# One meeting of the engines per stage instead of two, and the first pair of heads split one stage earlier, in a six-stage graph-attention and transformer kernel

## What is computed

```python
output = self_feat                              # [v, q] @ W_self.T + b_self
for d in range(2):
    output = output + _gat_attention(self_feat, cond, vb, Wq[d], bq[d], Wk[d], bk[d], Wout[d], bout[d])
x = v + relu(output)
mod = silu(c) @ W_mod + b_mod
sh_msa, sc_msa, g_msa, sh_mlp, sc_mlp, g_mlp = jnp.split(mod, 6, axis=-1)
x = x + g_msa * _attention(_modulate(_layernorm(x), sh_msa, sc_msa), W_qkv, W_out, b_out)
x = x + g_mlp * _ff(_modulate(_layernorm(x), sh_mlp, sc_mlp), W1, b1, W2, b2)
```

## Time and profile before

| What | Value |
|---|---|
| median of 3 runs | 3193.44 us (3193.24 to 3194.74) |
| the profiled execution | 3194.45 us |
| its span, first to last instruction | 3192.7 us |
| PE, PEld busy | 3071.8 us (96%), 2442.5 us (77%) |
| DVE, ACT, POOL busy | 1852.1 us (58%), 1341.3 us (42%), 845.3 us (26%) |
| mean granted TensorE clock | 0.981 |
| stages by first meeting | tables to 170.3, graph to 511.8, projections to 1062.5, attention to 2238.4, output projection to 2424.9, mlp to 3191.1 us |

### The profile page before, as it was taken

The page is one execution under the profiler, slowest core; times in us unless marked ns, Lnnn a source line. Parts: engine busy times, 40 slices in busy tenths (PEclk is TensorE's granted clock), DMA queues, the critical chain, the costliest instruction groups (busy, mean ns, idle before and its releaser), DMA issues. The chain is left out here.

```text
span 3192.7 us, 62151 instructions
## 1 busy us (share of the span) xinstructions
PE 3071.8 (96%) x24696; PEld 2442.5 (77%) x24696; DVE 1852.1 (58%) x2743; ACT 1341.3 (42%) x2786; POOL 845.3 (26%) x571
## 2 busy tenths in 40 slices
PE   8979998999999799999999999998996999999998
PEld 5969997888888577777777777776785888888887
DVE  4358982221211588888888888887674334343332
ACT  2146662222222377777777777776003111111111
POOL 1011213000000244434443444345455111111110
PEclk9989999999999899999999999999997999999999
DMA  4554322333332433333333333332663001000100
GB/s 141 176 186 149 117 79 99 106 105 114 113 106 93 102 107 92 91 100 81 88 94 100 81 88 88 102 87 68 221 232 112 1 27 33 26 33 26 33 14 14
DMA packets 196341, 297.28 MB, mean 93 GB/s; under 512 B 27888, under 2 KB 105712, under 8 KB 194054
## 3 DMA queue, kind: packets, MB, share of 16 engines
q1 hardware_dynamic: 182528, 276.54, 27.8%
q0 software_dynamic: 4288, 14.68, 1.3%
q10 hardware_dynamic: 9296, 2.77, 0.4%
HBM read 190.44 MB, written 103.49 MB: 92 GB/s over the span
## 5 line engine op out<-in xcount | busy, mean ns | idle before, releaser
L1339 DVE TENSOR_REDUCE b_nm<-b_ps 128x1 f32<-128x1024 f32 x512 | 602.0, 1217 | 16.6 <-PE b_ps L1280 3.4
L1246 ACT ACTIVATE b_p<-b_ps,b_nm 128x1024 f32<-128x1024 f32 x512 | 565.0, 1113 | 41.0 <-DVE b_nm L1339 41.0
L1309 PE MATMUL b_po<-b_pt,b_v 128*64 128x256 f32 x4096 | 498.3, 385 | 0.8 <-DVE b_pt L1359 0.8
L1251 ACT ACTIVATE b_pt<-b_tp_act 128x512 f32<-128x512 f32 x512 | 308.6, 603 | 306.4 <-PE b_tp_dve L1292 306.4
L1359 DVE COPY b_pt<-b_tp_dve 128x512 f32<-128x512 f32 x512 | 351.5, 687 | 117.9 <-PE b_tp_dve L1292 117.9
L1292 PEld LDWEIGHTS b_tp_act<-ident,b_p 64*128 64x128 f32 x4096 | 313.0, 139 | 129.7 <-issue 100.8
L1309 PEld LDWEIGHTS b_po<-b_pt,b_v 128*64 128x64 f32 x4096 | 271.8, 136 | 128.7 <-ACT b_pt L1251 0.9
L1292 PE MATMUL b_tp_act<-ident,b_p 64*128 64x64 f32 x4096 | 348.6, 225 | 2.4 <-issue 2.4
L1292 PE MATMUL b_tp_dve<-ident,b_p 64*128 64x64 f32 x4096 | 348.6, 225 | 0.0
L1701 ACT ACTIVATE d_ge<-d_pf,d_b 128x512 f32<-128x512 f32 x128 | 88.1, 689 | 596.7 <-PE d_pf L1723 596.7
L1292 PEld LDWEIGHTS b_tp_dve<-ident,b_p 64*128 64x128 f32 x4096 | 312.6, 139 | 1.6
(11 more groups left out here) (253 smaller groups left out, 5666.1 us busy)
## 6 DMA issues: line engine op xcount, KB each, us to landing
b_raw_q<-q_t SPq DMA_DIRECT2D x128, 256.0 KB, 4.1
q_t<-p_qk SPq DMA_DIRECT2D x64, 256.0 KB, 2.0
k_t<-p_qk SPq DMA_DIRECT2D x64, 256.0 KB, 2.0
v_n<-p_vs SPq DMA_DIRECT2D x32, 512.0 KB, 3.2
b_raw_k<-k_t SPq DMA_DIRECT2D x128, 128.0 KB, 4.2
b_v<-v_n SPq DMA_DIRECT2D x32, 512.0 KB, 3.9
b_rb<-inv SPq DMA_DIRECT2D x64, 256.0 KB, 3.8
o_t<-b_ot SPq DMA_DIRECT2D x32, 512.0 KB, 2.6
```

The source lines that it names most:

```text
L1246: act.activation(pr[k % 4][:], ps[k % 2][:], ACT.Exp, bias=nm[:, k % 4:k % 4 + 1], accum_out=rs[:, n:n + 1]).then_inc(exp_done, 1)
L1251: act.activation(dst, src, ACT.Copy).then_inc(t_out[0], 1)
L1309: mm = pe.matmul(po[rows, (blk % 2) * 2 * P:(blk % 2 + 1) * 2 * P], vt[u][:, kc, rows], pt[blk % 2][h][:, kc, :], start=(kc == 0), stop=(k ...
L1339: dve.tensor_reduce(nm[:, k % 4:k % 4 + 1], ps[k % 2][:], axis=AX.X, op=ALU.max, negate=True).then_inc(max_done, 1)
```

## The change

`sems()` no longer makes a second meeting. POOL clears the numbers in contiguous ranges right behind the block's own meeting, at the head of its program for the next stage, and the numbers are released so that the next stage takes others. Every block is opened with `no_gpsimd_drain=True`, so POOL's full drain is gone from the meeting. Because of that, the stores of `y` in `graph_attention` move from POOL's queue to SP's: SP issues the store of tile k - 4 ahead of the load of tile k, and waits for the last ones. In `projections`, SP loads q and k of pair 0 at the head of the last group (eight DMAs), DVE splits both heads there, ahead of that group's v copies, and the result stays in tiles `pair0` that `attention` uses as its first set. The load, the split and the wait on them at the start of `attention` are gone, with the semaphores `first_in` and `first_split`.

```diff
-def sems(ctx, nc, prefix, names, first=False):
+def sems(ctx, nc, prefix, names):
...
     def clear():
-        nc.clear_and_free_semaphores(handles)
-        if first:
-            nc.all_engine_barrier()
+        numbers = sorted(h.num for h in handles)
+        for low in [n for n in numbers if n - 1 not in numbers]:
+            high = low
+            while high in numbers:
+                high += 1
+            nc.gpsimd.sem_clear(range(low, high))
+        for h in handles:
+            nc.release_semaphore(h)
...
-        w_mod_in = sems(ctx, nc, "tables", "w_mod_in0 w_mod_in1")
-        block = ctx.enter_context(nc.Block())
+        w_mod_in = [nc.alloc_semaphore("tables_w_mod_in%d" % i) for i in range(2)]
+        for h in w_mod_in:
+            ctx.callback(nc.gpsimd.sem_clear, h)
+        block = ctx.enter_context(nc.Block(no_gpsimd_drain=True))
...
# graph_attention, SP
+            def store(k):
+                sp.wait_ge(y_done, k + 1)
+                sp.dma_start(y[k * P:(k + 1) * P, :], yo[k % 2][:]).then_inc(y_out[k % 2], 16)
+
             def turn(i):
                 for j in range(TT):
                     k = i * TT + j
+                    if k >= 4:
+                        store(k - 4)
                     sp.wait_ge(x_free, k + 1)
...
+            for k in range(B * BT - 4, B * BT):
+                store(k)
+            for n in range(2):
+                sp.wait_ge(y_out[n], 16 * B * BT // 2)
...
# graph_attention, POOL
-                pool.dma_start(y[k * P:(k + 1) * P, :], yo[k % 2][:]).then_inc(y_out[k % 2], 16)
...
-            for n in range(2):
-                pool.wait_ge(y_out[n], 16 * B * BT // 2)
...
# projections, SP
+            def load_pair0():
+                for h in range(2):
+                    for half in range(2):
+                        rows = slice(half * D1, (half + 1) * D1)
+                        sp.dma_start(raw_q[h][rows, :], q_t[0, h * D1:(h + 1) * D1, :]).then_inc(pair_in, 16)
+                        sp.dma_start(raw_k[h][rows, :], k_t[0, h * D1:(h + 1) * D1, half * S // 2:(half + 1) * S // 2]
+                                     ).then_inc(pair_in, 16)
...
+                    if last and hf:
+                        load_pair0()
...
# projections, DVE
+                    if not more:
+                        dve.wait_ge(pair_in, 128)
+                        for h in range(2):
+                            dve.tensor_copy(pair0["qh"][h][:], raw_q[h][:])
+                            dve.tensor_copy(pair0["kh"][h][:], raw_k[h][:]).then_inc(pair_rounded, 1)
+                            dve.wait_ge(pair_rounded, h + 1)
+                            dve.tensor_tensor(pair0["ql"][h][:], raw_q[h][:], pair0["qh"][h][:], ALU.subtract)
+                            dve.tensor_tensor(pair0["kl"][h][:], raw_k[h][:], pair0["kh"][h][:], ALU.subtract)
...
# attention
-        qh = [ring(ctx, nc, f"b_qh{u}", 2, [P, S], F32R) for u in range(2)]
+        qh = [pair0["qh"], ring(ctx, nc, "b_qh", 2, [P, S], F32R)]
...
-                for h in range(2):
-                    for half in range(2):
-                        sp.dma_start(raw_q[h][HALF[half], :], q_t[0, HALF[h], :]).then_inc(first_in[h], 16)
-                        sp.dma_start(raw_k[h][HALF[half], :], k_t[0, HALF[h], half * SK:(half + 1) * SK]
-                                     ).then_inc(first_in[h], 16)
...
-            pool.wait_ge(first_split, 4)
             pool.sem_inc(raw_used, 1)
...
-                if k in (0, 2):
-                    pe.wait_ge(first_split, k + 2)
-                elif s == 0:
+                if k and s == 0:
                     pe.wait_ge(qk_ready, i * TURN + k // STEPS)
...
-            for h in range(2):
-                dve.wait_ge(first_in[h], 64)
-                dve.tensor_copy(qh[0][h][:], raw_q[h][:])
-                dve.tensor_copy(kh[0][h][:], raw_k[h][:]).then_inc(first_split, 1)
-                dve.wait_ge(first_split, 2 * h + 1)
-                dve.tensor_tensor(ql[0][h][:], raw_q[h][:], qh[0][h][:], ALU.subtract)
-                dve.tensor_tensor(kl[0][h][:], raw_k[h][:], kh[0][h][:], ALU.subtract).then_inc(first_split, 1)
             maximum(0, 0)
```

More of the change, by code:

```diff
@@ L441, in graph_attention @@
             ctx, nc, "graph", "st_in ws_done zeros_set dve_step rs_done xt_done xh_copied xl_done o_done a_done adj_used lg_done sub_done "
-            "exp_done p_done wt_done wt_copied pv_done relu_done y_done x_free w_in", first=True)
+            "exp_done p_done wt_done wt_copied pv_done relu_done y_done x_free w_in")
         x_in = sems(ctx, nc, "graph", " ".join("x_in%d" % i for i in range(4)))
@@ L827, in norm_statistics, with projections @@
     dve.tensor_scalar(var_eps[:], mean_var[:, :, 1], EPS, None, ALU.add).then_inc(var_ready, 1)
-def projections(nc, t, ident, mod_t, y, q_t, k_t, v_n, wqk, x_first):
+def projections(nc, t, ident, mod_t, y, q_t, k_t, v_n, pair0, wqk, x_first):
     NQK = 2 * PAIRS
@@ L854, in projections @@
         vs = ring(ctx, nc, "p_vs", 2, [P, INNER], F32)
+        raw_q = ring(ctx, nc, "p_raw_q", 2, [P, S], F32)
+        raw_k = ring(ctx, nc, "p_raw_k", 2, [P, S // 2], F32)
         pt = banks(ctx, nc, "p_pt", 2)
@@ L859, in projections @@
             ctx, nc, "proj", "w_split ln_step half_set var_ready rstd_ready z_done t_done xm_done rounded x_split mb_done "
-            "m_done qk_done v_done w_rounded qk_free v_free", first=True)
+            "m_done qk_done v_done w_rounded qk_free v_free")
         w_in, ones_set = sems(ctx, nc, "proj", "w_in ones_set")
+        pair_in, pair_rounded = sems(ctx, nc, "proj", "pair_in pair_rounded")
         y_in = sems(ctx, nc, "proj", "y_in0 y_in1")
@@ L1059, in _, with attention @@
             turn(B - 1, True)
-def attention(nc, t, ident, q_t, k_t, v_n, inv, o_t, wo, wo_raw, o_first, o_first_raw):
+def attention(nc, t, ident, q_t, k_t, v_n, pair0, inv, o_t, wo, wo_raw, o_first, o_first_raw):
     STEPS = 2 * (S // P)
@@ L1089, in attention @@
         raw_k = ring(ctx, nc, "b_raw_k", 2, [P, SK], F32)
-        qh = [ring(ctx, nc, f"b_qh{u}", 2, [P, S], F32R) for u in range(2)]
-        ql = [ring(ctx, nc, f"b_ql{u}", 2, [P, S], F32R) for u in range(2)]
-        kh = [ring(ctx, nc, f"b_kh{u}", 2, [P, SK], F32R) for u in range(2)]
-        kl = [ring(ctx, nc, f"b_kl{u}", 2, [P, SK], F32R) for u in range(2)]
+        qh = [pair0["qh"], ring(ctx, nc, "b_qh", 2, [P, S], F32R)]
+        ql = [pair0["ql"], ring(ctx, nc, "b_ql", 2, [P, S], F32R)]
+        kh = [pair0["kh"], ring(ctx, nc, "b_kh", 2, [P, SK], F32R)]
+        kl = [pair0["kl"], ring(ctx, nc, "b_kl", 2, [P, SK], F32R)]
         vt = ring(ctx, nc, "b_v", 2, [P, BT, P], F32)
@@ L1409, in output_projection @@
         (rounded, o_split, m_done, gated_done, bias_done, y_bias, y_done) = sems(
-            ctx, nc, "outproj", "rounded o_split m_done gated_done bias_done y_bias y_done", first=True)
+            ctx, nc, "outproj", "rounded o_split m_done gated_done bias_done y_bias y_done")
         w1_in, = sems(ctx, nc, "outproj", "w1_in")
@@ L1570, in mlp @@
             "t_done xm_done rounded x_split f1_done gelu_done g_rounded g_split f2_done o_done gated_done "
-            "bias_done y_bias y_done", first=True)
+            "bias_done y_bias y_done")
         w2_in = sems(ctx, nc, "mlp", " ".join("w2_in%d" % i for i in range(NP2)))
@@ L1873, in split_pair @@
             return (high, rest), raw
+        first_pair = ExitStack()
         with ExitStack() as part:
@@ L1878, in program @@
             graph_attention(nc, t, ident, mod_t, gp, cg, pn, y, wqk, wqk_raw, x_first)
-            projections(nc, t, ident, mod_t, y, q_t, k_t, v_n, wqk, x_first)
+            pair0 = {name: [first_pair.enter_context(nc.sbuf_tensor(f"pair0_{name}{h}", [P, cols], F32R, side="right"))
+                            for h in range(2)] for name, cols in (("qh", S), ("ql", S), ("kh", S // 2), ("kl", S // 2))}
+            projections(nc, t, ident, mod_t, y, q_t, k_t, v_n, pair0, wqk, x_first)
         with ExitStack() as part:
@@ L1882, in program @@
             o_first, o_first_raw = split_pair(part, "o_first", [P, INNER // P, 512])
-            attention(nc, t, ident, q_t, k_t, v_n, inv, o_t, wo, wo_raw, o_first, o_first_raw)
+            attention(nc, t, ident, q_t, k_t, v_n, pair0, inv, o_t, wo, wo_raw, o_first, o_first_raw)
+            first_pair.close()
             w1_raw, w1l = over_raw(ctx, nc, "w1", [P, KC, MLP], top=True)
```

15 lines of the change are left out of this document (7 added, 8 removed).

## The result

The changed kernel takes 3182.16 us (median of 6 runs, 3179.73 to 3184.36) against 3194.23 us of the kernel before beside it; the ratio is 0.9962, interval 0.9949 to 0.9975. That is 12 us faster where 20.8 us were forecast, and outside the range of 3166.5 to 3178.5 us. The ratios differ from the quotients of the medians by up to 0.0004.

What follows compares the result with a forecast made beforehand. TensorE bounds each stage, so gains lie between stages: second meetings 1.2 + 1.6 + 1.2 + 1.2 + 1.2, graph end 3.5, attention start 10.4, program end 0.5, together 20.8 us; 3193.44 - 20.8 = 3172.6 us, range 3166.5 to 3178.5.

Steps and rivals of the forecast that it cites:

- Inside a stage nothing moves the end unless it makes TensorE wait: All stages: TensorE has no time left over inside them, so the time to be had lies between stages.
- The second meetings, 6.4 us: Five stage borders: dropping the second meeting gains 1.2 + 1.6 + 1.2 + 1.2 + 1.2 us.
- The end of the graph attention, 3.5 us: Graph attention's end: SP issues the last store right away, so the meeting comes 3.5 us sooner (3.0 to 3.9).
- absorbed: Graph attention tiles: SP's 0.33 us store issue ahead of x's load costs nothing, since ACT waits 2.6 us a tile.
- Its sentence on stores behind the 4 MB load: Graph attention, SP's queue: a store comes up to the 4 MB load's time later, without changing the sum.
- The start of the attention, 10.4 us: Attention's start: first maximum 2.2 us after the meeting instead of 12.6, gaining 10.4 us (9.5 to 11).
- The clock: Shortened stage gaps: same fall to half clock, return after as much dense work as now, 2 us or so either way.
- the first two rivals: Projections' and attention's starts: clock returns at its own time, 3178 us, chance 0.08; gap too short to fall, 3168 us, 0.07.
- The projections, nothing: Last group of the projections: SP's eight issues, 4.5 us, and DVE's split, about 6 us, cost nothing.
- The third: Attention's start hangs on something else, such as pair 1's loads or splits; half the 10.4 us comes: 3178 us, chance 0.07.
- the fourth: Graph attention: SP's queue delays rows of x, 1.6 us late a tile, at worst 51 us: 3224 us, chance 0.03.
- the fifth: Stage borders: the meeting waits for POOL anyway, so the second meetings give nothing: 3179 us, chance 0.05.

Runs made afterwards that it cites:

- Alone, with the code in place: One meeting per stage as the only change to the kernel before, plus 16 spare increments in TensorE's MLP opening: 3185.34 us, ratio 0.9967.
- the stores and drains alone: Kernel before with only y's graph attention stores on SyncE's queue and without GpSimd's drains at the stages' ends: 3192.73 us, ratio 0.9989.
- the parts alone: Kernel before with one part each: one meeting (0.9996; 0.9967 with 16 increments), first pair loaded and split early (0.9965), stores with missing drains (0.9989).
- The kernel with one increment: Changed kernel plus one spare semaphore increment, which nobody waits for, in TensorE's opening of the MLP: 3172.42 us, 0.9928 of the kernel before.
- 160 increments: 160 spare increments in TensorE's MLP opening: 3184.40 us on the changed kernel, 3204.63 us on the kernel before; laid where they cost nothing, changed kernel: 3172.43 us.
- kernel with six increments: Changed kernel plus six spare semaphore increments in TensorE's opening of the MLP: 3173.86 us, 0.9937 of the kernel before.

## Why the prediction was wrong, point by point

**Inside a stage nothing moves the end unless it makes TensorE wait.** This is the step that failed, at the very start. The sentence is true, and I then put the inside of the MLP at nothing, without a row, because no engine there got another instruction. I looked for waits on other engines only. The fetching of TensorE's own program was on no list: not as a term, not as a rival, not under "what would show it". It cost 8.7 us of the 9.6 by which the median missed the forecast; the opening's wait and half clock are another 1.2, and the other terms' errors nearly cancel.

**The second meetings, 6.4 us.** Right: 6.7 us of records are gone. Alone, with the code in place, that part measures 9.4 us by the medians, interval 6.4 to 14.4 (0.9980 to 0.9955 of 3194.7), so the term lies at the interval's edge; its profiled span is 7.2 us shorter.

**The end of the graph attention, 3.5 us.** The border is right to 0.05 us: from GpSimd's last addition to the release 5.99 us before, 2.53 after. The stage gained 2.5, since the last addition itself came 1.0 us later in it. The lateness begins at the fourth tile (0.7 us early at the third, 1.1 late at the fourth) and is partly made up by the ninth. From the third tile to the fourth it grows by 0.7 to 2.4 us in all nine kernels with the new stores and not at all in the four others without; at the last addition it is 2.1 us with the stores and drains alone, -0.1 to 2.5 over all nine, -0.5 to 0.6 without new stores. ScalarE's read of a row of x, just ahead of its part of the fourth tile, shows where it comes from, before and after:

```profile
235.28 0.62 ACT L560 ACTIVATE a_x_copy<-a_x 128x512 f32<-128x512 f32 x1
```

```profile
236.58 0.63 ACT L576 ACTIVATE a_x_copy<-a_x 128x512 f32<-128x512 f32 x1 [1.70 <-DMA a_x<-x]
```

The row was issued at 230.64 us and landed 3.2 us later before; after, it was issued at 231.09 us, 0.96 us behind a store of y, and took 5.5 us. That wait is there in all nine kernels with the new stores (0.7 to 2.3 us) and in none of the others. So "absorbed" and "cost nothing" were wrong at some tiles, for about 1 us in this profile, and the new wait of ScalarE for `a_x`, which the prediction named as a sign of being wrong, did come: ScalarE waits for rows of x six times instead of twice. Its sentence on stores behind the 4 MB load is borne out: the store issued at 241.58 us, behind the load of 231.97 us that took 15.3, landed after 6.4 us where the median is 2.1, and no engine's wait for it is recorded.

**The start of the attention, 10.4 us.** Mechanism and place are right: from release to first maximum 12.6 us before, 2.2 after, as worked out. The stage gained 11.8, and alone 13.1 (1161.6 us). The first pair of heads takes 36.1 us in place of 37.5, and that is the clock, which is back at full speed 8.4 us behind the release instead of 24.7. Over the kernels that share this start, the first pair takes 35.0 us where it is back after 3.6 us, 36.0 to 36.1 after 8.2 to 9.1, and 36.8 to 37.0 after 12.6 to 13.0. The stretch in the changed kernel:

```profile
1056.60:1066.80 10.20, 6.63 (x40) 4.79 (x40) 4.46 (x5) 2.41 (x4) 0.10 (x1) 0.50 0.81 206
```

**The clock.** As forecast it fell in both short gaps, and it came back after work, not at its own time: the half-clock stretch at the attention is 10.2 us long, against 27.3 before (1061.1 to 1088.4), and 10.2 against 13.7 at the projections (6.8 to 13.7 over the kernels with the change). That closes the first two rivals. The forecast's "after as much dense work as now" was not right, though: at the attention the clock was back 8.0 us after the first scores, where it had been 15.6 before. The Trainium skill, TensorE: Matmul & The Clock Gate, section Why this matters for your kernels, says that an idle TensorE drops to half its clock and gets it back by sustained work; the trace agrees. What I hadn't looked at is how little it takes: gaps of 2.24 and 2.75 us in a full MLP were each followed by a stretch of 3.4 us at half clock. Over all kernels here, ten gaps of 2.14 to 3.28 us in the MLP, at full clock until then, were followed by one, and ten of 1.26 to 2.26 us were not.

**The projections, nothing.** Right: 548.9 for 549.1 us, with the first pair's eight issues and its split inside. ScalarE waits once for SyncE there, 2.3 us, and TensorE for neither.

**The program's end, 0.5 us.** Right: 1.6 to 1.1 us.

**The tables, nothing.** They read 1.6 us longer, but over the kernels of this study they last 170.3 to 172.2 us with the change and 170.3 to 171.5 without. So 1.6 us in one profile can be spread; that the change costs nothing there isn't shown more closely than that.

**Rivals.** The third (half of the attention's gain), the fourth (rows of x late all along, 51 us) and the fifth (the meetings give nothing) are all refuted by the parts alone; of the fourth, single late rows did come. The result lay nearest to the fifth's time, 3179 us, for a reason that isn't in it.

**The range.** The bounds given for the terms, added up, reach from 3169.0 to 3177.3 us, and not from 3169.5 to 3176, and the fifth rival's 3179 us lies outside the 3178.5 us that were said to take it in. Neither would have held the result.

**What the forecast was worth.** Put back by one instruction, the same change takes 3172.42 us; the forecast was 3172.6. That it agrees to 0.2 us is in part luck: in that kernel's profile the attention gained 1.7 us more than forecast and the output projection 1.0 us, and the tables read 1.7 us longer. The kernel with one increment beats both kernels, by 0.72% and 0.3%.

## What to carry to other kernels

When an edit adds or removes instructions on an engine that runs a long loop, count the loop's instructions and where it starts against the engine's fetch blocks, and compare the instruction fetches of both profiles (one line of the queues) before anything else. An estimate from the seven blocks of 256 that this one loop of 1661 showed: a TensorE loop of some 1540 to 1790 instructions may fall either way, a shorter one always stays and a longer one never; of a loop that doesn't stay resident, see that its start isn't the last few instructions of a block, and a few spare increments, where the engine waits anyway, move it. An experiment that pads code must itself be read by stage: 160 increments cost about as much as the effect that they were to show, and the total alone agreed with a wrong reason.

## What the runs showed of the hardware

- TensorE keeps a loop that lies across seven blocks of 256 instructions (a branch back over 1661 of them takes 0.21 us, no fetches), and doesn't keep it across eight (3.3 to 3.9 us, 9 fetches a pass). The Trainium skill, Runtime: NRT & Kernel Launch, section Instruction fetch mechanics, gives blocks of 16 KiB, which the packets bear out, and says that a taken branch outside a window of two pages stalls; on TensorE the window was at least seven here.
- A fetch at a branch is hidden by products already queued, some 4 us of them; a second missing block right behind isn't. It cost 2.24 and 2.75 us of standstill with one instruction between, 2.14 and 2.26 with five, 1.61 and 1.26 with nine, none with 97, and 1.4 us more where the clock fell to half behind it.
- A semaphore increment on TensorE takes 0.154 us in a row of them.
- VectorE's cast and subtraction of 128x512 took 0.43 and 0.69 us alone, 1.92 and 2.71 us beside GpSimd's subtractions of 128x1024 (kernel with six increments). One of GpSimd's took 2.37 us alone and up to 2.86 us beside them (kernel with one increment).
- A 256 KB store on SyncE's queue landed after 2.1 us (median of 32), one on GpSimd's queue after 4.1 us.
